# Retention attention with routed experts: another order of the first 20 microseconds (loads, tile moments, first value product, warm-up)

## Chip, cores and metric

One core of one Trainium2 chip. The time is device microseconds of one launch, median of three runs. The matrix work is in float32; the warm-up and the routing one-hots are bfloat16.

## What is computed

Two sequences of 512 tokens with 256 features pass through one layer. Both branches read the normalised input, and both results are added to it:

```
x  = L0_attn_x                       # (2, 512, 256)
xn = _layernorm(x)
# attention: 16 heads of 16, no softmax, a decay per head
q, k, v = heads(xn @ wq.T), heads(xn @ wk.T), heads(xn @ wv.T)
scores = (q @ k.T) * SCALE * gamma_h ** (i - j) * (i >= j)
y = _layernorm(scores @ v, ln_w, ln_b)
attn = (y * silu(xn @ wg.T)) @ wo.T
# experts: 32, four per token, weights 1.8 * softmax(top 4 of the router's logits)
routed = sum_k rw_k * (silu(xn @ gate_e.T) * (xn @ up_e.T)) @ down_e.T
shared = (silu(xn @ sg.T) * (xn @ su.T)) @ sd.T
out = x + attn + routed + shared
```

## The kernel before

The 1024 tokens are 8 tiles of 128, four to a sequence (CPB). The program is written by hand for each engine: every engine runs its own list in order, and semaphores tie the lists together. An instruction that waits holds everything behind it in its own list.

The start. SyncE issues the loads of x in five pieces (HEAD: tile 0, tile 1, then pairs 2-3, 4-5, 6-7; L461), the q/k weights and the v/gate weights (L465, L466), the decay table of 1 MB (`dec`, L469) and the constants (L470). TensorE runs warm-up matmuls on ones (L1353), which produce nothing that is used. VectorE takes each tile's moments (`moments` L924, `aggregate` L927, `scale_moments` L936 and L937), GpSimd raises the variance to the power -1/2 (`token_scale`, L845), VectorE refines the root (L916 to L918) and normalises the tile (L930). Tiles 0 and 1 go one at a time; tiles 2 to 7 have one aggregate, one power and one refinement together. TensorE transposes the normalised tiles (`transpose_tokens`, L1368) and ScalarE copies them to `xnT` (`take_features`, L559).

Each tile t then passes through: `project_qk` (L1430) and `project_vg` (L1440); `scores` (L1455), four PSUM banks r = 0 to 3 with two heads' groups each; `decay_scores` on VectorE (L1095), one product with the decay table for each r; `weigh_values` (L1505), the value product, which reads the decayed scores `st` and the spread values `vz`; `transpose_keys` (L1468) and `decay_keys` (L1102); `chunk_products` (L1481) and `update_state` (L1111) for the state carried to the next tile; `transpose_outputs` (L1514). TensorE interleaves tile t's value product with tile t+1's projections.

GpSimd's list at the start is: two one-tile powers, two memsets, the power for tiles 2 to 7, two casts of constants (L853, L854, after the constants have landed), then `spread_values(0)` (L834), which makes `vz` for tile 0:

```
            token_scale(2, slice(2, NT))
            pool.wait_ge(c2_in, 16)
            nc.gpsimd.tensor_copy(iota_bf[:, :], cst[:, C_IO:C_IO + P])
            nc.gpsimd.tensor_copy(lt_bf[:, :], cst[:, C_LT:C_LT + P]).then_inc(pool_cst, 1)
            spread_values(0)
```

`weigh_values(t)` waits for both of its inputs:

```
                pe.wait_ge(sc_sb, 4 * t + 4)
                pe.wait_ge(vz_sb, 2 * (t + 1))
```

After tile 1's scores come the router's logits over all 1024 tokens (`router_logits`, L1378, which needs all of `xnT`), a ScalarE copy (L573), and two transposes back (`transpose_logits`, L1386). VectorE then picks the experts, and tokens are sorted into blocks beside the attention tiles until about 84 us. The expert pairs run from there to about 178 us, and the weighted sum of the routed rows ends the program.

## Time and profile before

| what | value |
|---|---|
| median of 3 runs | 205.25 us (204.96 to 206.94) |
| profiled execution | 205.5 us |
| its span in the trace | 203.7 us |
| granted TensorE clock | 1.0 of full speed on average |

The trace's time starts with the span. The 1.8 us between the span and the profiled execution's time lie around the program. In rows of the timeline a number after x counts instructions merged into one row, and the bracket gives the engine's idle time before it and what ended it; PE is TensorE's matmuls, PEld its weight loads, DVE VectorE, ACT ScalarE, POOL GpSimd, SPq SyncE's queue. Float32 matmuls appear as several passes, so a row's count can be twice or four times the program's.

### The profile page before, as it was taken

To read this page: it belongs to the slowest core of one execution; us is meant where nothing else is said; L and a number is where in the kernel's file an instruction comes from. 1 tells how busy PE (TensorE), PEld (TensorE's weight loads), DVE (VectorE), ACT (ScalarE), POOL (GpSimd) and SP (SyncE) were. 2 spreads that over 40 slices of the span, in tenths; PEclk is the share of its full clock that TensorE was granted. 3 is DMA by queue.
4 is the path that set the end of the run, shared out by engine and by line. 5 is a ranking of instruction groups with operands and counts; after the bars stand their busy time and mean duration, and the time that the engine had idled before them with its cause. 6 is when DMAs were issued, how large, how long until landed. Compare 5 with 4: busy or idle time off the path is not lost.

```text
span 203.7 us, 4593 instructions
## 1 busy us (share of the span) xinstructions
PE 193.9 (95%) x1594; PEld 143.2 (70%) x1594; DVE 118.6 (58%) x362; ACT 95.1 (47%) x241; POOL 112.1 (55%) x156
## 2 busy tenths in 40 slices
PE   8999998999879999989999999999999999999984
PEld 2666766778466858788888668777866786587653
DVE  2577789798979876764333422433342333415895
ACT  2046247645759242653238547634925931125300
POOL 1234047524984768677777777777777533630000
PEclk9999999999999999999999999999999999999999
DMA  4993999997000029999957334324333333217993
GB/s 124 335 359 130 330 425 427 429 427 344 5 0 0 5 63 393 385 354 396 373 194 266 104 101 146 91 87 146 106 102 105 117 124 142 100 54 237 352 312 131
DMA packets 18551, 42.36 MB, mean 208 GB/s; under 512 B 2517, under 2 KB 11098, under 8 KB 17760
## 3 DMA queue, kind: packets, MB, share of 16 engines
q1 hardware_dynamic: 14640, 33.03, 44.6%
q0 software_dynamic: 3456, 8.92, 13.2%
q8 instruction: 13, 0.21, 0.4%
q10 hardware_dynamic: 432, 0.12, 0.3%
q14 instruction: 10, 0.08, 0.1%
HBM read 34.71 MB, written 7.86 MB: 209 GB/s over the span
## 4 chain that ended last, share of the span: by engine, by line
PE 65%; DVE 10%; POOL 7%; DMA 7%; ACT 4%; issue 4%; SPq 2%; POOLq 0%; DVEq 0%
PE bank L1565 19%; PE bank L1578 6%; DMA w_mem<-y_rows 5%; PE bank L1582 4%; PE bank L1543 4%; PE bank L1353 4%; DVE w_mem L1095 4%; PE bank L1430 4%; PE bank L1440 3%; PE bank L1505 3%; PE bank L1602 3%; PE bank L1455 3%; PE bank L1531 3%; POOL y_rows L823 2%; POOL xg_mem L801 2%
## 5 line engine op out<-in xcount | busy, mean ns | idle before, releaser
L1565 PE MATMUL bank<-xb_mem,w_mem 128*128 128x128 f32 x384 | 47.8, 276 | 0.1
L823 POOL DMA_INDIRECT y_rows<-y_mem,codes x36 | 36.2, 1007 | 18.5 <-DVE y_mem L1158 9.7
L1565 PEld LDWEIGHTS bank<-xb_mem,w_mem 128*128 128x128 f32 x384 | 45.2, 192 | 1.2 <-issue 0.9
L815 POOL DMA_INDIRECT xg_mem<-xn_rows,codes x36 | 35.4, 984 | 12.9 <-issue 9.4
L1150 DVE TENSOR_TENSOR h_mem<-h_mem,bank 128x128 f32<-128x128 f32 x32 | 9.2, 287 | 42.2 <-ACT h_mem L629 41.9
L1095 DVE TENSOR_TENSOR w_mem<-bank,w_mem 128x512 f32<-128x512 f32 x32 | 20.1, 684 | 4.5 <-PE bank L1455 4.4
L1158 DVE COPY y_mem<-bank 128x256 f32<-128x256 f32 x36 | 13.9, 420 | 10.8 <-PE bank L1582 9.5
L628 ACT ACTIVATE h_mem<-bank 128x128 f32<-128x128 f32 x32 | 8.9, 277 | 23.7 <-PE bank L1565 23.4
L641 ACT COPY w_mem<-w_mem 128x1024 f32 x16 | 16.0, 1041 | 3.5 <-PE bank L1620 2.4
L1578 PE MATMUL bank<-w_mem,h_mem 128*128 128x256 f32 x60 | 16.1, 391 | 0.0
L1430 PE MATMUL bank<-w_mem 128*128 128x128 f32 x128 | 15.7, 276 | 0.0
L618 ACT COPY xb_mem<-bank 128x512 f32<-128x512 f32 x16 | 9.3, 584 | 13.6 <-PE bank L1543 12.9
L1430 PEld LDWEIGHTS bank<-w_mem 128*128 128x128 f32 x128 | 15.0, 192 | 0.5 <-issue 0.3
L1440 PE MATMUL bank<-w_mem 128*128 128x512 f32 x32 | 15.1, 593 | 0.0
L1578 PEld LDWEIGHTS bank<-w_mem,h_mem 128*128 128x128 f32 x60 | 10.3, 190 | 4.6 <-DVE h_mem L1152 2.5
L1769 PE MATMUL bank<-xg_mem,ws_mem 128*128 128x256 f32 x48 | 11.1, 385 | 0.0
L567 ACT ACTIVATE w_mem<-bank,cst 128x256 f32<-128x256 f32 x16 | 6.7, 470 | 9.5 <-PE bank L1430 9.4
L772 POOL TENSOR_TENSOR w_mem<-w_mem,cst 128x256 f32<-128x256 f32 x6 | 4.7, 790 | 11.4 <-ACT w_mem L569 11.3
L1582 PE MATMUL bank<-w_mem,h_mem 64*128 64x256 f32 x60 | 10.5, 428 | 0.0
L1543 PE MATMUL bank<-cst,xg_mem 128*128 128x128 f32 x64 | 10.4, 285 | 0.0
L1769 PEld LDWEIGHTS bank<-xg_mem,ws_mem 128*128 128x128 f32 x48 | 8.9, 190 | 2.2 <-issue 0.7
L1304 DVE SCALAR_TENSOR_TENSOR x_sb<-w_mem,rw,x_sb 128x256 f32<-128x256 f32 x22 | 9.4, 480 | 1.5 <-DMA w_mem<-y_rows 1.4
(171 smaller groups left out, 326.0 us busy)
## 6 DMA issues: line engine op xcount, KB each, us to landing
w_mem<-w_exp_dram SPq DMA_DIRECT2D x3, 3456.0 KB, 21.6
w_mem<-w_late_dram SPq DMA_DIRECT2D x7, 1152.0 KB, 7.2
w_mem<-y_rows SPq DMA_DIRECT2D x8, 512.0 KB, 8.0
w_mem<-w_qkvg_dram SPq DMA_DIRECT2D x2, 512.0 KB, 6.2
w_mem<-decay_dram SPq DMA_DIRECT2D x1, 1024.0 KB, 8.2
xn_rows<-w_mem SPq DMA_DIRECT2D x2, 512.0 KB, 3.5
xnt_rows<-w_mem SPq DMA_DIRECT2D x1, 1024.0 KB, 4.9
w_mem<-w_ovf_dram SPq DMA_DIRECT2D x16, 64.0 KB
```

Source lines behind the costliest of these rows:

```text
L641: return nc.scalar.copy(o_mem[:, j * OW:j * OW + XW], w_mem[:, bass.ds(e * EW, XW)])
L815: nc.gpsimd.indirect_dma_start(xg[:, k % RING, :], None, xn_rows, bass.IndirectOffsetOnAxis(ap=codes[:, c, 0:1], axis=0),).then_inc(tok_in ...
L823: nc.gpsimd.indirect_dma_start(y_rows, bass.IndirectOffsetOnAxis(ap=codes[:, c, 1:2], axis=0), ysb[:, k % YRING, :], None, bounds_check=RO ...
L1095: nc.vector.tensor_tensor(st[:, 4 * r * P:4 * (r + 1) * P], ps_s[r][:, :], dec[:, 4 * r * P:4 * (r + 1) * P], ALU.mult).then_inc(sc_sb, 1)
L1158: nc.vector.tensor_copy(ysb[:, w, :], ps[:, 0:D]).then_inc(ys_sb, 1)
L1430: last = nc.tensor.matmul(ps_qk[:, m * P:(m + 1) * P], wqkvg[:, g, m * P:(m + 1) * P], tokens(g, t), start=(g == 0), stop=(g == KT - 1))
L1440: last = nc.tensor.matmul(ps_vg[:, :], tokens(g, t), wqkvg[:, g, 2 * D:4 * D], start=(g == 0), stop=(g == KT - 1))
L1543: last = nc.tensor.transpose(ps_xt[p % 2][:, (2 * g + j) * P:(2 * g + j + 1) * P], xg[:, k % RING, g * P:(g + 1) * P], ident)
L1565: last = nc.tensor.matmul(ps_gu[j][:, m * P:(m + 1) * P], w[:, o:o + P], xbT[:, p % 2, (2 * g + j) * P:(2 * g + j + 1) * P], start=(g == 0 ...
L1578: nc.tensor.matmul(ps_dn[j][:, 0:D], hA[:, 2 * (p % 2) + j, :], w[:, j * EW + KT * MB:j * EW + XW], start=True, stop=False)
L1582: nc.tensor.matmul(ps_dn[j][:, 0:D], hC[rows, p % 2, :], w2[rows], start=False, stop=True).then_inc(dn_ps, 1)
L1769: last = nc.tensor.matmul(to, ws_mem[:, o:o + P], xnT_back[:, g, n], start=(g == 0), stop=(g == KT - 1))
```

## The change

- Warm-up: 17 matmuls become 15 ahead of the first transposes, and behind them 5 (17 // 3) become 2 (15 // 7).
- SyncE issues the decay table after tiles 2-3 of x, ahead of tiles 4 to 7.
- VectorE takes the moments of tiles 2 and 3, then decays the score banks 0 and 1 of tile 0, then does the moments of tiles 4 to 7 with the aggregates and scales of tiles 2 to 7, then banks 2 and 3, then the refinement and all six normalisations.
- TensorE does the first value product and tile 0's key transposes ahead of the transposes of tiles 2 to 5; tiles 6-7 are transposed behind tile 1's scores; the router's logits go behind the chunk products.
- The transposes of tiles 2 to 7 write other PSUM banks, with waits to match. Two waits for feature copies ahead of the value product and the key transposes go.
- ScalarE's list follows: its three feature copies stand together behind `take_outputs(0)`.

GpSimd's list is not touched.

```diff
--- before.py
+++ after.py
@@ -58,7 +58,7 @@
 DVE_ROWS = {n: (0, 1, 2, 3) for n in range(5)} | {5: (2, 3)}
 PE_ROWS = ((5, 0), (5, 1), (6, 0), (6, 1), (6, 2), (6, 3), (7, 0), (7, 1), (7, 2), (7, 3))
 PE_TILES = (5, 6, 7)
-WARM_UP = 17
+WARM_UP = 15
 CT = 32
 
 
@@ -297,7 +297,7 @@
         bank = [ctx.enter_context(nc.psum_tensor(f"bank{i}", [P, 512], F32)) for i in range(8)]
         ps_tr, ps_qk, ps_vg, ps_sg, ps_s0, ps_s1, ps_y, ps_po = bank
         ps_s = [ps_s0, ps_s1, ps_sg, ps_tr]
-        ps_f = [ps_s0, ps_s1, ps_y, ps_po, ps_qk]
+        ps_f = [ps_s0, ps_s1, ps_qk, ps_vg, ps_qk]
 
         ps_xt, ps_gu, ps_dn, ps_og, ps_ot = [ps_qk, ps_vg], [ps_s0, ps_s1], [ps_sg, ps_tr], ps_y, ps_po
         ps_sa, ps_sc, ps_sd = ps_xt, ps_gu, [ps_dn, [ps_og, ps_ot]]
@@ -464,9 +464,10 @@
             tokens_in(1)
             sp.dma_start(wqkvg[:, :, 0:2 * D], w_qkvg[:, :, 0:2 * D]).then_inc(wqk_in, 16)
             sp.dma_start(wqkvg[:, :, 2 * D:4 * D], w_qkvg[:, :, 2 * D:4 * D]).then_inc(wvg_in, 16)
-            for u in range(2, len(HEAD)):
-                tokens_in(u)
+            tokens_in(2)
             sp.dma_start(dec[:, :], decay).then_inc(d_in, 16)
+            tokens_in(3)
+            tokens_in(4)
             sp.dma_start(cst[:, C_BM:C_END], consts[:, C_BM:C_END]).then_inc(c2_in, 16)
             sp.dma_start(wo[:, :, :], w_out).then_inc(w_in, 16)
             sp.dma_start(lnw[:, :], lnwb[0].partition_broadcast(P)).then_inc(w_in, 16)
@@ -692,16 +693,14 @@
                     take_output_tokens(t - 1)
                 hot_positions(t, "tok")
                 take_queries_keys(t + 1)
-                if t == 0:
-                    take_features(2)
-                    take_features(3)
                 if t >= 2:
                     take_transposed(t - 2)
                 hot_positions(t, "z")
                 take_values_gate(t + 1)
                 take_outputs(t)
                 if t == 0:
-                    take_features(4)
+                    for u in range(2, len(HEAD)):
+                        take_features(u)
                 if t == T_RANK + 1:
                     hot_positions(t, "y")
                 if 1 <= t < T_EXPERT:
@@ -946,13 +945,17 @@
             normalise(0)
             refine(1, slice(1, 2))
             normalise(1)
-            for t in range(2, NT):
-                last = moments(t)
-            step(last)
-            for t in range(2, NT):
-                last = aggregate(t)
-            step(last)
-            scale_moments(slice(2, NT))
+            moments(2)
+            step(moments(3))
+
+            def rest_of_moments():
+                for t in range(4, NT):
+                    last = moments(t)
+                step(last)
+                for t in range(2, NT):
+                    last = aggregate(t)
+                step(last)
+                scale_moments(slice(2, NT))
 
             def take_logits():
                 dve.wait_ge(lg_ps, 1)
@@ -1205,13 +1208,12 @@
                         make_codes()
                         find_block_experts()
                     decay_scores(t, r)
-                    if t == 0 and r == 0:
-                        refine(2, slice(2, NT))
-                        for u in range(2, 6):
-                            normalise(u)
+                    if t == 0 and r == 1:
+                        rest_of_moments()
                 if t == 0:
-                    normalise(6)
-                    normalise(7)
+                    refine(2, slice(2, NT))
+                    for u in range(2, NT):
+                        normalise(u)
                 if t == T_RANK - 1:
                     take_logits()
                 if t % CPB > 0 and t < NT - 1:
@@ -1360,8 +1362,12 @@
             def transpose_tokens(u):
 
                 pe.wait_ge(xn_done, HEAD[u][-1] + 1)
+                if u == 2:
+                    pe.wait_ge(qk_sb, 2)
+                if u == 3:
+                    pe.wait_ge(vg_sb, 4)
                 if u == 4:
-                    pe.wait_ge(qk_sb, 2)
+                    pe.wait_ge(xnT_sb, 3)
                 for g in range(KT):
                     for j, t in enumerate(HEAD[u]):
                         o = (len(HEAD[u]) * g + j) * P
@@ -1459,8 +1465,6 @@
                             last.then_inc(sc_ps, 1)
 
             def transpose_keys(t):
-                if t == 0:
-                    pe.wait_ge(xnT_sb, 4)
                 if t >= 2:
                     pe.wait_ge(res_sb, t - 1)
                 need(pe, st_sb, states_before(t))
@@ -1493,8 +1497,6 @@
                                      qd[:, t % 2, g * P:(g + 1) * P], start=(g == 0), stop=False, skip_group_check=True)
 
             def weigh_values(t):
-                if t == 0:
-                    pe.wait_ge(xnT_sb, 3)
                 pe.wait_ge(sc_sb, 4 * t + 4)
                 pe.wait_ge(vz_sb, 2 * (t + 1))
                 for g in range(KT):
@@ -1683,7 +1685,7 @@
                     transpose_back(NT - 1)
 
             transpose_tokens(0)
-            warm_up(WARM_UP // 3)
+            warm_up(WARM_UP // 7)
             pe.wait_ge(xnT_sb, 1)
             pe.wait_ge(wqk_in, 16)
             project_qk(0)
@@ -1698,7 +1700,7 @@
                 if t >= 1:
                     scores(t)
                 if t == 1:
-                    router_logits()
+                    transpose_tokens(4)
                 if t == T_INVERT:
                     route_inverse()
                 if not more:
@@ -1706,6 +1708,8 @@
                     transpose_pair(0)
                 if t % CPB > 0:
                     chunk_products(t - 1)
+                if t == 1:
+                    router_logits()
                 if t >= 1:
                     transpose_outputs(t - 1)
                 if t == 1:
@@ -1723,16 +1727,14 @@
                 if t >= 2 and more:
                     transpose_back(t - 2)
                 from_state(t)
-                if t == 0:
-                    transpose_tokens(2)
-                    transpose_tokens(3)
                 if t >= 2 and more:
                     project_out(t - 2)
                 weigh_values(t)
                 if t % CPB < CPB - 1:
                     transpose_keys(t)
                 if t == 0:
-                    transpose_tokens(4)
+                    transpose_tokens(2)
+                    transpose_tokens(3)
 
             pe.wait_ge(vg_sb, 2 * NT)
             transpose_pair(1)
```

TensorE, from tile 1's v/gate projection to the logits' transposes, before:

```order
L1440 MATMUL bank<-w_mem 128x512 x2
L1368 MATMUL bank<-cst,w_mem 128x128 x8
L1505 MATMUL bank<-w_mem 32x128 x16
L1468 MATMUL bank<-cst,w_mem 128x128 x2
L1368 MATMUL bank<-cst,w_mem 128x128 x4
L1455 MATMUL bank<-w_mem 128x256 x8
L1378 MATMUL bank<-w_mem 32x256 x8
L1481 MATMUL bank<-w_mem 128x128 x2
L1514 MATMUL bank<-cst,w_mem 128x128 x2
L1386 MATMUL bank<-cst,w_mem 128x128 x2
```

The same stretch of TensorE's list in the changed kernel (L1446 is the v/gate projection, L1507 the value product, L1472 the key transposes, L1374 the transposes of x, L1461 scores, L1485 chunk products, L1384 logits, L1516 outputs, L1392 logits back):

```order
L1446 MATMUL bank<-w_mem 128x512 x2
L1507 MATMUL bank<-w_mem 32x128 x16
L1472 MATMUL bank<-cst,w_mem 128x128 x2
L1374 MATMUL bank<-cst,w_mem 128x128 x8
L1461 MATMUL bank<-w_mem 128x256 x8
L1374 MATMUL bank<-cst,w_mem 128x128 x4
L1485 MATMUL bank<-w_mem 128x128 x2
L1384 MATMUL bank<-w_mem 32x256 x8
L1516 MATMUL bank<-cst,w_mem 128x128 x2
L1392 MATMUL bank<-cst,w_mem 128x128 x2
```

The eight transposes of tiles 2 to 5 moved from ahead of the value product to behind it, the four of tiles 6-7 to behind the scores, and the logits to behind the chunk products.

VectorE, from the moments of tile 2 to tile 0's decayed keys, before:

```order
L924 BN_STATS w_mem<-x_sb 128x6 x6
L927 BN_AGGR w_mem<-w_mem 128x2 x6
L936 TENSOR_SCALAR w_mem<-w_mem 128x6
L937 TENSOR_SCALAR w_mem<-w_mem 128x6
L1095 TENSOR_TENSOR w_mem<-bank,w_mem 128x512
L916 TENSOR_TENSOR w_mem<-w_mem 128x6
L917 TENSOR_TENSOR w_mem<-w_mem 128x6
L918 SCALAR_TENSOR_TENSOR w_mem<-w_mem 128x6
L930 TENSOR_SCALAR w_mem<-x_sb,w_mem 128x256 x4
L1095 TENSOR_TENSOR w_mem<-bank,w_mem 128x512 x3
L930 TENSOR_SCALAR w_mem<-x_sb,w_mem 128x256 x2
L1102 TENSOR_TENSOR w_mem<-bank,cst 128x256
```

The same stretch in the changed kernel (L923 moments, L1098 decays, L926 aggregates, L935 and L936 scales, L915 to L917 the refinement, L929 the normalisations):

```order
L923 BN_STATS w_mem<-x_sb 128x6 x2
L1098 TENSOR_TENSOR w_mem<-bank,w_mem 128x512 x2
L923 BN_STATS w_mem<-x_sb 128x6 x4
L926 BN_AGGR w_mem<-w_mem 128x2 x6
L935 TENSOR_SCALAR w_mem<-w_mem 128x6
L936 TENSOR_SCALAR w_mem<-w_mem 128x6
L1098 TENSOR_TENSOR w_mem<-bank,w_mem 128x512 x2
L915 TENSOR_TENSOR w_mem<-w_mem 128x6
L916 TENSOR_TENSOR w_mem<-w_mem 128x6
L917 SCALAR_TENSOR_TENSOR w_mem<-w_mem 128x6
L929 TENSOR_SCALAR w_mem<-x_sb,w_mem 128x256 x6
L1105 TENSOR_TENSOR w_mem<-bank,cst 128x256
```

Two decays now stand ahead of the aggregates and scales, and no normalisation stands between the decays.

## Rows read from the trace of the kernel before

**Rows 1.** The page, part 4: engines on the chain that ended last.

```profile
PE 65%; DVE 10%; POOL 7%; DMA 7%; ACT 4%; issue 4%; SPq 2%; POOLq 0%; DVEq 0%
```

**Rows 2.** Timeline, TensorE, start to first projection: start us, us, engine, line, op.

```profile
0.96 6.78 PE L1353 MATMUL bank<-w_mem 128*128 128x512 bf16 x17 [0.96 <-POOL w_mem L839]
...
6.91 0.34 PEld L1353 LDWEIGHTS bank<-w_mem 128*128 128x128 bf16 x2 [0.28 <-issue]
...
7.58 0.38 PE L1368 MATMUL bank<-cst,w_mem 128*128 128x128 f32 x2
...
7.80 1.24 PE L1353 MATMUL bank<-w_mem 128*128 128x512 bf16 x5
...
8.88 1.95 PE L1430 MATMUL bank<-w_mem 128*128 128x128 f32 x16
```

**Rows 3.** Timeline, TensorE, from the first scores to tile 2's projection.

```profile
12.69 1.15 PE L1455 MATMUL bank<-w_mem 32*128 32x256 f32 x16
...
17.37 1.04 PE L1368 MATMUL bank<-cst,w_mem 128*128 128x128 f32 x8
...
18.65 1.09 PE L1505 MATMUL bank<-w_mem 128*32 128x128 f32 x32 [0.24 <-ACT w_mem L559]
...
19.94 0.60 PE L1368 MATMUL bank<-cst,w_mem 128*128 128x128 f32 x4
...
20.47 1.15 PE L1455 MATMUL bank<-w_mem 32*128 32x256 f32 x16
...
21.55 1.07 PE L1378 MATMUL bank<-w_mem 128*32 128x256 f32 x16
...
23.10 0.38 PE L1514 MATMUL bank<-cst,w_mem 128*128 128x128 f32 x2
...
23.53 1.95 PE L1430 MATMUL bank<-w_mem 128*128 128x128 f32 x16
```

**Rows 4.** Timeline, VectorE.

```profile
9.65 2.29 DVE L924 BATCH_NORM_STATS2 w_mem<-x_sb 128x6 f32<-128x256 f32 x6 [1.86 <-DMA x_sb<-x_dram]
...
13.96 0.69 DVE L1095 TENSOR_TENSOR w_mem<-bank,w_mem 128x512 f32<-128x512 f32 x1 [1.20 <-PE bank L1455]
...
15.24 1.38 DVE L930 TENSOR_SCALAR w_mem<-x_sb,w_mem 128x256 f32<-128x256 f32 x4
...
21.64 2.48 DVE L1095 TENSOR_TENSOR w_mem<-bank,w_mem 128x512 f32<-128x512 f32 x4 [1.07 <-PE bank L1455]
...
29.14 0.42 DVE L1102 TENSOR_TENSOR w_mem<-bank,cst 128x256 f32<-128x256 f32 x1 [0.56 <-PE bank L1468]
```

**Rows 5.** Timeline, GpSimd, from the third power to the first value spread.

```profile
12.91 1.33 POOL L845 TENSOR_TENSOR w_mem<-w_mem 128x6 f32<-128x6 f32 x1 [6.17 <-DVE w_mem L937]
...
14.89 0.29 POOL L853 CAST w_mem<-cst 128x128 bf16<-128x128 f32 x1 [0.65 <-DMA cst<-consts_dram]
...
15.37 0.76 POOL L834 COPY w_mem<-w_mem 128x128 f32<-128x128 f32 x2
```

**Rows 6.** Timeline, ScalarE, three copies out of PSUM.

```profile
8.00 0.37 ACT L559 COPY w_mem<-bank 128x256 f32<-128x256 f32 x1 [5.37 <-PE bank L1368]
...
20.58 0.58 ACT L559 COPY w_mem<-bank 128x512 f32<-128x512 f32 x1 [0.40 <-PE bank L1368]
...
22.68 0.37 ACT L573 COPY w_mem<-bank 128x256 f32<-128x256 f32 x1 [1.52 <-PE bank L1378]
```

**Rows 7.** Timeline, SyncE's queue: two of the loads issued at the start.

```profile
1.63 0.68 SPq L465 DMA_DIRECT2D w_mem<-w_qkvg_dram  x1
...
5.68 0.66 SPq L469 DMA_DIRECT2D w_mem<-decay_dram  x1
```

**Rows 8.** The page, part 6: DMA issues, KB each, median us to landing.

```profile
w_mem<-w_qkvg_dram SPq DMA_DIRECT2D x2, 512.0 KB, 6.2
...
w_mem<-decay_dram SPq DMA_DIRECT2D x1, 1024.0 KB, 8.2
```

**Rows 9.** Timeline, TensorE: its longest idle stretch before 66 us.

```profile
57.41 0.44 PE L1468 MATMUL bank<-cst,w_mem 128*128 128x128 f32 x2 [1.60 <-DVE x_sb L1126]
```

## The prediction

> **What bounds the kernel now.** I read the chain that ended last first: 65% of it is TensorE [rows 1]. Then I read the timeline of the first 30 us engine by engine, since the whole change lies there. TensorE's rows run nearly end to end: warm-ups and projections [rows 2], then scores at 12.69, transposes at 17.37, the first value product at 18.65, and so on to tile 2's projection at 23.53 [rows 3]. The reader should see that almost no row of TensorE has an idle time in its bracket; the one with 0.24 us is the first value product, held by a ScalarE copy. Last, VectorE sits idle for 0.56 us at 29.14 until TensorE's key transposes of tile 1 arrive [rows 4], and the routing work hangs on VectorE from there. So what TensorE loses or gains before 29 us goes into the end. I measure each case by when tile 2's projection starts, 23.53 before.
>
> **The start, 0.73 us earlier.** From 0.96 to 7.58 TensorE issues 17 matmuls of 512 columns [rows 2]. At 1.2 GHz one takes 0.427 us, at 2.4 GHz 0.213 us; 6.62 us are 14 at the lower clock and 3 at the upper. So the two that go would have run at the upper clock: 0.43 us, and the transposes start at 7.15. Tile 0 is normalised by then, since its copy would otherwise not have followed the transposes so closely: it starts 0.42 us after them and takes 0.37 [rows 6]. Now 7.15 + 0.42 + 0.37 = 7.94, and with some 0.2 for the signal and the weight load the first projection starts at 8.15. Before it started at 8.88, right behind the five warm-ups of 7.80 [rows 2]; two of them now end at 7.8 and don't hold it. Its weights were issued at 1.63 [rows 7] and land 6.2 us later [rows 8], at 7.8: just in time. Gain 8.88 - 8.15 = 0.73. Scores of tile 0 move from 12.69 to 11.96.
>
> **The decay load.** Issued at 5.68 [rows 7], it lands after 8.2 us [rows 8], at 13.88, and the first decay starts at 13.96 [rows 4]. Tile 1's decays start 1.17 us after its scores (20.47 to 21.64, [rows 3, 4]), so tile 0's could have started at 13.86. The load cost only 0.1 before, but with scores 0.73 earlier it would eat the gain. Ahead of 512 KB of x it lands sooner: the last tiles of x had landed when their moments were taken, about 11.2 (9.65 + 4 x 0.38), so the table behind them took 2.7 us to 13.88; counted from 9.65, when tiles 2-3 are in [rows 4], it is there by about 12.4. I take it as no longer late. Tiles 4 to 7 then land by 13.9 at the latest, the end of the same bytes before, and are wanted at 14.4.
>
> **The new wait.** The value product needs the spread values. The spread stands on GpSimd behind the power for tiles 2 to 7, and that power needs the moments of all of them [rows 5]. Before, this was done at 15.37 + 0.76 = 16.13, well ahead of TensorE. Now the moments of tiles 4 to 7 come behind two decays. Step by step:
> - first decay at 11.96 + 1.17 = 13.13; two decays at 2.48/4 = 0.62 each [rows 4]: 14.37
> - four moments at 2.29/6 = 0.38 [rows 4]: 15.90
> - aggregates, scales and the signal: from the moments' end before, 9.65 + 2.29 = 11.94, to the power at 12.91 [rows 4, 5], 0.97: 16.87
> - the power, 1.33: 18.20. The two casts, 15.37 - 14.89 = 0.48, with the constants long landed, plus 0.05: 18.73
> - the spread, 0.76 [rows 5]: 19.49, and 0.1 for the signal: the value product starts at 19.6, against 18.65.
>
> TensorE is through tile 1's projections at 17.37 - 0.73 = 16.64, so it stands still for nearly 3 us with the transposes, the scores and all else queued behind it. VectorE's banks 2 and 3, done at 16.9 + 1.25 = 18.1, are not the last wait. That is +0.95.
>
> **From the value product to tile 2's projection.** Before this took 23.53 - 18.65 = 4.88 [rows 3]. Now the transposes of tiles 2 to 5 are in it: eight transposes at 0.11 us, since the four of 19.94 are done some 0.44 later, ahead of the scores at 20.47 [rows 3]: +0.88. Are their inputs ready at about 20.8? The refinement starts with the power's end, 18.3, and takes under 0.7; normalisations go at 1.38/4 = 0.35 each [rows 4]: tile 3 at 19.7, tile 5 at 20.4, tile 7 at 21.1. Yes, by a few tenths; this costs nothing.
>
> Tiles 6-7 are transposed behind tile 1's scores. Before, transposes at 19.94 led to a copy at 20.58 of 0.58 [rows 3, 6], hidden under the scores. Now the logits come only the chunk products later: the copy's end is 0.64 + 0.58 + 0.05 = 1.27 after the transposes' start, and transposes and chunk products fill 0.44 + 0.5 (from 21.55 to 23.10 are logits and chunk products, 1.55, less 1.05). Wait +0.33. The logits' own copy ends 22.68 + 0.37 - 21.55 = 1.50 after the logits start, with the signal 1.65; before, chunk products and output transposes covered it, now logits and output transposes fill 1.05 + 0.22. Wait +0.38. Bounds of the two together: 0 if they stay hidden, 1.0 if ScalarE is late with them; I take 0.71, which the rows give.
>
> **Sum.** 0.95 + 0.88 + 0.33 + 0.38 = +2.54 at tile 2's projection; the gain of 0.73 and the lost 0.24 stall are already in the 0.95. VectorE's path to 29 us is late too, but less: the logits reach it at about 26.3 instead of 24.04, +2.3. So TensorE's +2.54 holds at 29.14 and is carried on. The profiled execution, 205.5, becomes 208.0; it lies 0.25 over the median, so the median becomes 207.8. Bounds of the new wait: GpSimd's spans are called rough by the page. If they are much too long, VectorE's fourth decay at 18.1 is the last wait, the value product starts at 18.2 and the sum is 1.1. If normalisations or spread slow each other, another 0.5 comes on top.
>
> **Rivals.**
> (a) The wait is small: GpSimd's chain is really a microsecond or more shorter, or the two copies stay hidden. For it: the power of six columns was never on the chain, so its true end is bounded only by VectorE's use of it. Against it: a decrease of more than 1.4 us is not to be had. Result +1.1 to +1.9, 206.4 to 207.1: within 1%. It decides if the spread ends before 19.0.
> (b) TensorE's clock falls in the gap. The longest idle stretch before 66 us is 1.60 us [rows 9], and what follows it runs at the upper of the two levels; the new gap is nearly 3 us, which no row here covers. If the clock fell and stayed down as long as at the start (0.96 to about 6.9, 5.9 us), the work in that time would run at half speed: at most +3.0, together 210.8. The Trainium skill (TensorE: Matmul & The Clock Gate, "Why this matters for your kernels") warns that idle gaps between bursts of matmuls bring the clock back to its half rate. By that rule the sum would be 210.8; the trace agrees only in that shorter gaps do no harm.
> (c) Not slower: the delay is taken up behind 29 us and the earlier start stays. For that VectorE or TensorE would have to have some 2.5 us of slack in the routing stage. TensorE has idle time there, 1.60 us at 57.41 [rows 9], and if the same work could slide into it, and the last waits there were not for this stage's start, the kernel would come out at 205.25 - 0.73 = 204.5. It decides from the point at which VectorE stops being fed late. Against it: the chain runs through VectorE's idle 0.56 us at 29.14 straight to TensorE, and later idle times are waits for VectorE's own chain, which shifts with it.
> (d) The change doesn't do what it says: the value product is first on TensorE's list, but isn't first in time since it still waits for the moments. That is what I forecast. If instead its inputs were there when TensorE comes, at 16.7, tile 2's projection would start at 16.7 + 4.88 + 0.88 + 0.71 = 23.17, 0.4 early: 204.9. The fourth decay at 18.1 alone excludes that.
>
> **How the numbers follow.** The forecast (+2.0 to +3.3) gets 0.65, (a) 0.2, (b) 0.1, (c) and (d) together 0.05. Both of these end within 1% too; a gain of over 1% has no mechanism here, and 0.02 is left for it. A measurement of this kernel tells about 1%, 2.05 us, from no change: the line is 207.3. Within the forecast some 0.05 lies under the line, the rest above; with (b) slower is 0.70, within 1% is 0.28, faster 0.02. The range goes from 206.4, the low end of (a), to 210.2, over half of (b).
>
> **What would show it.** In the changed trace: first projection near 8.2; first decay near 13.1; the power on GpSimd near 16.9, the spread's end near 19.5; the value product at 19.6 with an idle bracket of nearly 3 us that names GpSimd; logits with 0.3 us of idle and the logits' transposes with 0.4; tile 2's projection near 26.1; VectorE's decayed keys of tile 1 near 31.7; everything behind by 2.5. I am wrong if the value product starts before 18.7, if matmuls behind the gap take twice their time, or if the later stages don't shift with the first.

## The result, and the profile after

| | before | changed |
|---|---|---|
| median | 205.4 us (6 runs, 204.96 to 206.94) | 209.24 us (6 runs, 207.43 to 209.46) |
| ratio | | 1.0172, interval 1.0138 to 1.0206 |
| profiled execution, its span | 205.5, 203.7 | 209.17, 207.3 |

The changed kernel is slower by 1.7%. Ratios, here and below, leave out executions more than 1.5% above the fastest of their kernel; medians and ranges keep them. The timeline of the changed kernel on TensorE, with the columns of [rows 2] and [rows 3]:

```profile
0.96 5.53 PE L1355 MATMUL bank<-w_mem 128*128 128x512 bf16 x15 [0.96 <-POOL w_mem L838]
...
6.80 0.41 PE L1374 MATMUL bank<-cst,w_mem 128*128 128x128 f32 x2 [0.31 <-DVE w_mem L929]
...
7.67 2.05 PE L1436 MATMUL bank<-w_mem 128*128 128x128 f32 x16
...
11.58 1.15 PE L1461 MATMUL bank<-w_mem 32*128 32x256 f32 x16
...
18.82 1.87 PE L1507 MATMUL bank<-w_mem 128*32 128x128 f32 x32 [2.39 <-POOL w_mem L833]
...
21.10 1.65 PE L1374 MATMUL bank<-cst,w_mem 128*128 128x128 f32 x8
...
22.69 1.15 PE L1461 MATMUL bank<-w_mem 32*128 32x256 f32 x16
...
25.14 1.07 PE L1384 MATMUL bank<-w_mem 128*32 128x256 f32 x16 [0.28 <-issue]
...
26.69 0.44 PE L1392 MATMUL bank<-cst,w_mem 128*128 128x128 f32 x2
...
26.97 1.95 PE L1436 MATMUL bank<-w_mem 128*128 128x128 f32 x16
```

The first projection starts at 7.67 (8.88 before, [rows 2]), the first scores at 11.58 (12.69, [rows 3]): the start did get faster, by 1.21 and 1.11 us. Then the value product stands behind 2.39 us of idle time that the row puts down to GpSimd's L833, the value spread. The value product starts at 18.82, hardly later than the 18.65 of before. But tile 2's projection starts at 26.97 against 23.53. And one row is odd: the same 32 passes of the value product take 1.87 us, where before they took 1.09 [rows 3].

VectorE, which answers to [rows 4]:

```profile
12.81 1.29 DVE L1098 TENSOR_TENSOR w_mem<-bank,w_mem 128x512 f32<-128x512 f32 x2 [2.86 <-PE bank L1461]
...
14.02 1.39 DVE L923 BATCH_NORM_STATS2 w_mem<-x_sb 128x6 f32<-128x256 f32 x4
...
18.49 2.44 DVE L929 TENSOR_SCALAR w_mem<-x_sb,w_mem 128x256 f32<-128x256 f32 x6
...
32.57 0.42 DVE L1105 TENSOR_TENSOR w_mem<-bank,cst 128x256 f32<-128x256 f32 x1 [1.29 <-PE bank L1472]
```

The first two decays, then the four moments without a wait, so both the table and tiles 4 to 7 had landed. The normalisations end only at 20.9. VectorE's key decay of tile 1 stood at 29.14 before and stands at 32.57 now, with 1.29 us of idle time in place of 0.56. I call this row "the keys" and use it as the measure of the first stage below: +3.43.

GpSimd, which answers to [rows 5]:

```profile
16.38 1.33 POOL L844 TENSOR_TENSOR w_mem<-w_mem 128x6 f32<-128x6 f32 x1 [9.87 <-DVE w_mem L936]
...
17.67 0.28 POOL L852 CAST w_mem<-cst 128x128 bf16<-128x128 f32 x1
...
18.15 0.52 POOL L833 COPY w_mem<-w_mem 128x128 f32<-128x128 f32 x2
```

The power runs at 16.38 (12.91 before), and the spread behind it at 18.15 (15.37 before). Last, busy time in four stretches, the start and three around the gap: us, each engine's busy time, TensorE's granted clock (PEclk), DMA.

```profile
core 0: us, PE busy (x) PEld busy (x) DVE busy (x) ACT busy (x) POOL busy (x), PEclk, DMA share, GB/s
0.00:5.40 5.40, 4.44 (x11) 1.64 (x12) 1.97 (x11) 1.50 (x3) 1.41 (x8) 1.00 0.53 139
...
16.30:18.80 2.50, 0.13 (x1) 0.01 (x1) 2.07 (x6) 0.66 (x2) 2.42 (x6) 1.00 0.00 0
...
18.80:22.60 3.80, 3.78 (x42) 3.33 (x42) 2.56 (x7) 0.77 (x2) 1.32 (x3) 0.55 0.55 181
...
22.60:26.90 4.30, 3.91 (x46) 2.54 (x45) 2.48 (x4) 1.99 (x5) 0.00 (x0) 1.00 0.52 198
```

In the 2.5 us ahead of the value product TensorE was all but idle. In the 3.8 us behind it, the granted clock was 0.55 of full speed, which is the lower of the two levels, 1.2 GHz, for nearly all of that stretch, and then 1.00 again. In the kernel before no stretch up to 28.7 us shows less than 1.00. The column is to be read beside durations: it says 1.00 for the first 5.4 us too, where 11 warm-ups took 4.44 us, 0.40 each, nearly the prediction's 0.427 for the lower level. Behind the gap column and durations agree (1.87 against 1.09). The six executions of the changed kernel show this too: five have a mean clock of 0.99 (0.990 to 0.992) and take 209.17 to 209.46 us; the sixth has 0.999 and takes 207.43.

So there are two parts: work that starts late, and a clock that is down behind the gap.

### The profile page after: what moved, and what is told of

The parts are those of the page before. It is cut to its first block, busy times and chain, and to the rows that moved or that the text cites. A ratio compares the mean times of both kernels' runs of the same rounds, so it can differ in the third digit from the quotient of the medians.

```text
span 207.3 us, 4585 instructions
## 1 busy us (share of the span) xinstructions
PE 194.3 (94%) x1589; PEld 143.8 (69%) x1589; DVE 118.8 (57%) x362; ACT 95.4 (46%) x241; POOL 112.3 (54%) x156
## 4 chain that ended last, share of the span: by engine, by line
PE 69%; DVE 16%; POOL 6%; ACT 4%; issue 2%; DMA 1%; ACTq 0%; DVEq 0%; POOLq 0%
PE bank L1567 20%; PE bank L1580 7%; PE bank L1771 5%; PE bank L1584 5%; DVE w_mem L1098 4%; PE bank L1545 4%; PE bank L1507 3%; PE bank L1604 3%; PE bank L1436 3%; PE bank L1461 3%; DVE x_sb L1306 3%; PE bank L1446 2%; PE bank L1533 2%; POOL xg_mem L800 2%; ACT xg_mem L585 2%
## 5 line engine op out<-in xcount | busy, mean ns | idle before, releaser
L1098 DVE TENSOR_TENSOR w_mem<-bank,w_mem 128x512 f32<-128x512 f32 x32 | 20.1, 683 | 7.2 <-PE bank L1461 7.1
L1580 PE MATMUL bank<-w_mem,h_mem 128*128 128x256 f32 x60 | 16.1, 392 | 0.0
L1446 PE MATMUL bank<-w_mem 128*128 128x512 f32 x32 | 15.1, 593 | 0.0
L1580 PEld LDWEIGHTS bank<-w_mem,h_mem 128*128 128x128 f32 x60 | 10.3, 190 | 4.6 <-DVE h_mem L1155 2.5
L1507 PE MATMUL bank<-w_mem 128*32 128x128 f32 x256 | 9.5, 292 | 2.7 <-POOL w_mem L833 2.4
L1507 PEld LDWEIGHTS bank<-w_mem 128*32 128x32 f32 x256 | 7.2, 115 | 5.4 <-issue 4.8
```

The source lines that it names most:

```text
L1098: nc.vector.tensor_tensor(st[:, 4 * r * P:4 * (r + 1) * P], ps_s[r][:, :], dec[:, 4 * r * P:4 * (r + 1) * P], ALU.mult).then_inc(sc_sb, 1)
L1446: last = nc.tensor.matmul(ps_vg[:, :], tokens(g, t), wqkvg[:, g, 2 * D:4 * D], start=(g == 0), stop=(g == KT - 1))
L1507: last = nc.tensor.matmul(ps_y[CT * r:CT * (r + 1), g * P:(g + 1) * P], vz[:, t % 2, h * CT:(h + 1) * CT], st[:, s * P:(s + 1) * P], start ...
L1580: nc.tensor.matmul(ps_dn[j][:, 0:D], hA[:, 2 * (p % 2) + j, :], w[:, j * EW + KT * MB:j * EW + XW], start=True, stop=False)
```

## The experiments

Each changes one thing in the changed kernel (names that begin with a) or in the kernel before (b); x are mixtures. "Value product", "projection" (tile 2's) and "keys" (VectorE's key decay of tile 1) are start times in the profiled execution.

| kernel | value product | projection | keys | median us | ratio to before |
|---|---|---|---|---|---|
| before | 18.65 | 23.53 | 29.14 | 205.2 | |
| changed | 18.82 | 26.97 | 32.57 | 209.2 | 1.0172 |
| a_spread_first | 17.61 | 26.88 | 32.49 | 207.66 | 1.0130 (1.0091 to 1.0169) |
| a_fill_gap | 18.84 | 25.39 | 30.99 | 208.47 | 1.0161 (1.0118 to 1.0203) |
| a_moments_early | 17.69 | 24.84 | 30.45 | 207.14 | 1.0094 (1.0068 to 1.0120) |
| a_old_loads | 19.39 | 27.56 | 33.16 | 209.82 | 1.0211 (1.0156 to 1.0265) |
| b_warm_loads | 21.56 | 26.44 | 32.05 | 209.30 | 1.0179 (1.0135 to 1.0223) |
| b_warm | 18.23 | 23.12 | 28.73 | 205.11 | 1.0001 (0.9963 to 1.0040) |
| b_loads | 21.11 | 27.54 | 33.15 | 210.50 | 1.0222 (1.0154 to 1.0289) |
| x_order | 16.24 | 22.81 | 28.42 | 205.77 | 1.0017 (0.9996 to 1.0038) |
| a_spread_fill2 | 17.65 | 25.52 | 31.12 | 208.50 | 1.0164 (1.0094 to 1.0234) |

### The spread ahead of the power (a_spread_first)

```diff
+            spread_values(0)
             token_scale(2, slice(2, NT))
             pool.wait_ge(c2_in, 16)
...
-            spread_values(0)
```

> The changed kernel with one edit: GpSimd spreads tile 0's values ahead of the power for tiles 2 to 7. Theory (the value product is held by GpSimd's list, and TensorE's clock falls in the gap): the spread is done by about 13, the value product now waits only for the fourth decay and starts at 17.4 to 17.6 instead of 18.8, the idle stretch ahead of it shrinks from 2.4 us to about 1.2, the granted clock stays at 1.0, and the transposes of tiles 2 and 3 wait some tenths for their normalisation. Time 206.3 to 207.0, some 1.5 us over the kernel before. Rival (the loss comes from the transposes and logits standing later on TensorE's list, and the gap is only where it shows): 208.5 to 209.2.

Measured 207.66, and on TensorE, in a view that ends at 21 us (so five of the eight transposes' passes):

```profile
17.61 1.09 PE L1507 MATMUL bank<-w_mem 128*32 128x128 f32 x32 [1.05 <-DVE w_mem L1098]
...
18.63 0.44 PE L1472 MATMUL bank<-cst,w_mem 128*128 128x128 f32 x2
...
19.95 1.31 PE L1374 MATMUL bank<-cst,w_mem 128*128 128x128 f32 x5 [0.89 <-DVE w_mem L929]
```

The value product is released by VectorE's decay at 17.61, as expected, and runs at full speed. But the transposes of tiles 2 and 3 now wait 0.89 us for a normalisation, and in the profiled execution the clock fell there, at 20.0 (1.83 us for tile 1's scores, 1.08 before): the profiled execution took 209.19, with a mean clock of 0.992, the other three 207.56 to 207.66 with 1.0. The median lies between the two forecasts, 0.7 above the theory's 206.3 to 207.0 and 0.8 below the rival's 208.5. The three executions with the clock held compare with the 207.43 of the changed kernel's one such execution: no gain. And with the clock held by fill, the keys come at 30.99 without this edit and at 31.12 with it (a_fill_gap and a_spread_fill2, below): the spread's place on GpSimd by itself is worth nothing. The late power holds the normalisations just as it held the spread, and the wait moves by one step. The gain in the median goes with the clock, which was down in one of four executions here and in five of six in the changed kernel. That is too few to show that two short gaps bring it down less often than one long gap.

### Matmuls in the gap (a_fill_gap)

```diff
+                if t == 0:
+                    warm_up(11)
                 weigh_values(t)
```

> The changed kernel with 11 warm-up matmuls of 512 columns (2.35 us at the upper clock) put ahead of tile 0's value product, where TensorE stood still for 2.4 us. They write a bank that the value product then starts anew. Theory (the gap lets the clock fall): the value product still starts at 18.8, but the granted clock holds 1.0 from there on, the 32 passes of the value product take 1.09 us instead of 1.87, and the time is 207.3 to 207.7, some 1.6 us under the changed kernel. Rival (the passes behind the gap are long for another reason, such as memory traffic of the normalisations beside them): 209.0 to 209.6, with the same long passes.

The chain of work that ended last (start us, us, what), four pieces:

```profile
16.46 2.37 PE bank L1355 x11
...
18.84 1.09 PE bank L1507 x32
...
20.30 0.87 PE bank L1374 x8
...
30.99 0.42 DVE w_mem L1105
```

and the stretch behind the gap, with the columns of the changed kernel's above:

```profile
18.80:22.60 3.80, 3.79 (x63) 3.06 (x63) 2.84 (x8) 1.45 (x3) 1.35 (x3) 1.00 0.54 179
```

The clock is 1.00, the value product takes 1.09, the eight transposes' passes 0.87 (in the changed kernel's chain 1.45), and the keys come at 30.99, 1.58 us earlier than in the changed kernel. Only fill was added, so the idle gap is what the lower clock goes with, and the price is 1.6 us, close to the 1.8 between the two kinds of executions of one kernel (209.2 and 207.4). One of the four executions, 209.86, still has a mean clock of 0.992; no trace shows where it fell.

The time missed its bracket of 207.3 to 207.7: it was 208.47, and the ratio, 1.0161, is not told apart from the changed kernel's 1.0172. In the profiled execution the keys' gain is there, but TensorE then loses 0.8 us of it in the expert stage, in two steps:

```profile
85.85 0.63 PE L1545 MATMUL bank<-cst,xg_mem 128*128 128x128 f32 x4 [0.43 <-issue]
...
174.25 0.42 DVE L1161 COPY y_mem<-bank 128x256 f32<-128x256 f32 x1 [0.67 <-DMA y_rows<-y_mem,codes]
...
174.82 1.10 PE L1580 MATMUL bank<-w_mem,h_mem 128*128 128x256 f32 x4 [0.16 <-DVE y_mem L1161]
```

The same pair of VectorE's copies in the changed kernel, without a wait for a DMA between them:

```profile
174.35 0.76 DVE L1161 COPY y_mem<-bank 128x256 f32<-128x256 f32 x2 [1.16 <-PE bank L1584]
```

Counted from the inversion of the routing (TensorE's L1418, 69.93 here, 71.49 in the changed kernel), TensorE's rows come 0.38 us later than the changed kernel's from 86 us on, and 0.77 later from 174.8 on. The second step is a VectorE copy of an expert result that waits for the write of an earlier result to `y_rows`, and TensorE's L1580 waits for that copy.

### The moments in their old place (a_moments_early)

```diff
-            moments(2)
-            step(moments(3))
-
-            def rest_of_moments():
-                for t in range(4, NT):
+            for t in range(2, NT):
...
-                    if t == 0 and r == 1:
-                        rest_of_moments()
```

> The changed kernel with VectorE's moments, aggregates and scales of tiles 2 to 7 all ahead of the first decay again, as before the change; TensorE's new order, loads and warm-up stay. Theory (the moved moments are what holds the value product): the spread is done at about 16, the value product starts at 16.3 to 16.5 with no idle time, tile 2's projection at about 22.8 against 23.5 before; time 204.3 to 205.0. Rival (TensorE's new order costs by itself, through the extra work ahead of tile 2's projection and the two exposed copies): 206 to 207.

Measured 207.14, 2.1 us over the top of the theory's bracket, with the clock held in all four executions (0.998 or 1.0). VectorE and TensorE (a view that ends at 20 us):

```profile
12.79 1.48 DVE L923 BATCH_NORM_STATS2 w_mem<-x_sb 128x6 f32<-128x256 f32 x4 [2.48 <-DMA x_sb<-x_dram]
...
17.69 1.09 PE L1501 MATMUL bank<-w_mem 128*32 128x128 f32 x32 [1.17 <-POOL w_mem L833]
...
19.33 0.97 PE L1368 MATMUL bank<-cst,w_mem 128*128 128x128 f32 x5 [0.18 <-DVE w_mem L929]
```

VectorE waits 2.48 us for tiles 4 and 5 of x, until 12.79. Before the change the six moments ran from 9.65 without a wait [rows 4]. The loads, not the moments' place, make it late: the decay table now goes ahead of these tiles. With the clock held on both sides this edit gains little: 207.14 against 207.43, and 30.45 against 30.99 at the keys.

### Warm-up and loads in the kernel before (b_warm_loads), and each alone (b_warm, b_loads)

```diff
-WARM_UP = 17
+WARM_UP = 15
...
-            for u in range(2, len(HEAD)):
-                tokens_in(u)
+            tokens_in(2)
             sp.dma_start(dec[:, :], decay).then_inc(d_in, 16)
+            tokens_in(3)
+            tokens_in(4)
...
-            warm_up(WARM_UP // 3)
+            warm_up(WARM_UP // 7)
```

> The kernel before with only the shorter warm-up and the decay table loaded ahead of tiles 4 to 7. Theory (the start is worth what TensorE's list shows, 0.7 to 1.2 us, and is carried to the end): 204.2 to 204.7. Rival (a wait that comes back takes the gain, such as a load or the decays): 205.2 to 205.5.

It took 209.3, which neither side expected: two edits that I had taken for gains, and as slow as the whole change. Its four executions go from 208.44, with a mean clock of 0.999, to 211.88 with 0.976. The profiled one is that with the clock held, although TensorE stood idle for 2.24 and 1.18 us in it, with 1.3 us of transposes between: the late tiles, without the clock, make it 3.2 us slower. The two were then run apart, with the hunk of the loads alone and that of the warm-up alone.

> The kernel before with the shorter warm-up alone. Theory (the load order is what cost 3 us when warm-up and loads were changed together): no harm; the first projection starts 0.7 to 1.2 us earlier, but the decay table still lands at 13.9, the first decay stays there and the value product starts at 18.3 to 18.6, so the time is 204.8 to 205.3. Rival (the shorter warm-up is what cost, since the matrix engine starts its work too soon or at a lower clock): 207 to 209.

> The kernel before with the decay table loaded ahead of tiles 4 to 7 alone. Theory: tiles 4-5 land at 12.8 to 13.3 instead of before 10.5, VectorE, which takes their moments ahead of everything, stands still for some 2.5 us, the six normalisations and the transposes behind them come late, tile 2's projection starts at 26 to 26.5; time 207.8 to 208.6. Rival (warm-up to blame): 205.1 to 205.6.

b_loads, at 210.5:

```profile
12.86 1.49 DVE L925 BATCH_NORM_STATS2 w_mem<-x_sb 128x6 f32<-128x256 f32 x4 [2.51 <-DMA x_sb<-x_dram]
...
18.63 1.30 PE L1369 MATMUL bank<-cst,w_mem 128*128 128x128 f32 x8 [1.77 <-DVE w_mem L931]
...
21.11 1.94 PE L1506 MATMUL bank<-w_mem 128*32 128x128 f32 x32 [1.18 <-ACT w_mem L560]
```

Moments 2.51 us late for want of x, transposes late by 1.77 us of idle time, and behind them the value product again at the lower clock (1.94 us). It is 1.9 us over the bracket of 207.8 to 208.6; I had not counted the clock, which accounts for most of it by the price found above. In the profiled execution (211.02, a mean clock of 0.983) the clock was down a second time, behind a gap of the same length as the one of [rows 9]:

```profile
61.46 0.44 PE L1469 MATMUL bank<-cst,w_mem 128*128 128x128 f32 x2 [1.60 <-DVE x_sb L1127]
...
61.83 1.87 PE L1456 MATMUL bank<-w_mem 32*128 32x256 f32 x16
```

The scores take 1.87 us here and 1.15 in the kernel before, and the granted clock is 0.54 from 61.8 to 65.5 us. b_warm, at 205.11:

```profile
7.82 2.05 PE L1430 MATMUL bank<-w_mem 128*128 128x128 f32 x16
...
13.67 0.69 DVE L1095 TENSOR_TENSOR w_mem<-bank,w_mem 128x512 f32<-128x512 f32 x1 [1.01 <-DMA w_mem<-decay_dram]
...
18.23 1.09 PE L1505 MATMUL bank<-w_mem 128*32 128x128 f32 x32 [0.78 <-ACT w_mem L559]
```

The first projection is 1.06 us earlier, but the first decay waits for the table (DMA), and the value product for ScalarE; 0.42 us is left at the value product, 0.41 at the keys, and nothing that can be measured at the end. So the warm-up is harmless and worth nothing that the medians show, and the load order alone costs as much as the whole change where VectorE wants tiles 4 to 7 first (1.0222 against 1.0172, with intervals that overlap).

### The changed kernel with the old loads (a_old_loads)

The hunk of the loads taken back.

> The changed kernel with the decay table loaded behind tiles 4 to 7, as before. Theory: the first decay starts at 13.9 instead of 12.8, and since the moments, the power and the spread follow it, the value product starts at 19.9 behind a gap of 3.6 us, with the clock fallen; time 210.0 to 210.6. Rival (the load order is hidden either way): 209.0 to 209.5.

```profile
13.38 1.29 DVE L1097 TENSOR_TENSOR w_mem<-bank,w_mem 128x512 f32<-128x512 f32 x2 [3.22 <-DMA w_mem<-decay_dram]
...
19.39 1.09 PE L1506 MATMUL bank<-w_mem 128*32 128x128 f32 x32 [3.10 <-POOL w_mem L832]
...
22.46 1.96 PE L1460 MATMUL bank<-w_mem 32*128 32x256 f32 x16
```

Measured 209.82, 0.2 below the bracket. The first decay does wait for the table, 13.38 instead of 12.81, and the gap is 3.10 us. The clock fell again, though not at once: the value product has its 1.09 us, tile 1's scores take 1.96. So with the moments late, the early table is worth 0.6 us at the keys (32.57 against 33.16, both with the clock down; in the times, 209.2 and 209.8, the intervals overlap); with the moments early it costs, as a_moments_early and b_loads show. The load order and the moments' place have to be chosen together.

### TensorE's order with the old loads and moments (x_order, x_hidden)

x_order is the changed kernel with the loads and the moments back in their old places, and the spread ahead of the power; TensorE's order and the short warm-up stay.

> The changed kernel's warm-up and TensorE order, with the loads and VectorE's moments in their old places and the value spread ahead of the power on GpSimd. Theory (each wait of the changed kernel comes from the loads, the moved moments and GpSimd's queue; TensorE's order itself costs the two exposed copies of 0.7 us): the moments are through at 12.5, the value product waits for the fourth decay and starts at 16.5, the granted clock stays at 1.0, tile 2's projection at about 23.1; time 204.5 to 205.2. Rival (TensorE's order costs 1.5 us by itself): 206 to 206.8.

The chain, three pieces:

```profile
14.59 1.72 PE bank L1439 x4
...
16.31 1.02 PE bank L1500 x32
...
28.42 0.42 DVE w_mem L1100
```

No gap at all: TensorE goes from tile 1's projections straight into the value product at 16.3, and the keys are at 28.42, 0.72 us ahead of the kernel before. The first stage went as the theory had it (the projection 0.3 early). The time did not: 205.77, not told apart from the kernel before, and 0.6 over the top of the bracket. From the keys on, this kernel takes some 0.2 us longer to the inversion of the routing (38.97 us against 38.72). The rest isn't lost in the profiled execution, which at 205.10 is the fastest of the ten: the shared experts' first matmul comes at 177.46 against 177.91, and the span is 203.2 against 203.7. What makes the other nine slower (205.42 to 205.99, clocks of 0.998 to 1.0) no trace shows.

This run takes out the late moments, the loads and the spread's place together, so it shows that they hold nearly the whole loss, and not the share of each. For TensorE's new order it leaves at most some tenths (1.0017, interval 0.9996 to 1.0038).

x_hidden also put the transposes of tiles 6-7 and the logits back where they were.

> The kernel of the run x_order with the transposes of tiles 6-7 ahead of tile 1's scores and the logits ahead of the chunk products, as before the change, so that ScalarE's two copies are covered again. Theory (the changed TensorE order costs 0.7 us in exposed copies): tile 2's projection starts at 22.1 to 22.3 instead of 22.8, VectorE's key decay of tile 1 at 27.8 to 28.0 against 29.1 in the kernel before; time 204.2 to 204.9, 0.3 to 0.8 us under the kernel before. Rival (gains of the first 30 us don't reach the end): 205.0 to 205.7.

The keys came at 28.39, no earlier than in x_order: the copies are covered again, but the transposes wait for the normalisations instead, and the gain is gone. Its time (231.17) says nothing, since the chip of this batch ran every kernel some 26 us longer, with stops behind 78 us, the kernel before included (231.9); the first 31 us of the profiles of this batch agree with those of other chips.

### Fill again (a_fill_8, a_spread_fill, a_spread_fill2)

a_fill_8 has 8 matmuls where a_fill_gap has 11; a_spread_fill is a_spread_first with 5 ahead of the value product and 4, to another PSUM bank, ahead of the transposes.

> The changed kernel with 8 warm-up matmuls (1.7 us) ahead of the value product, where 11 stood before: TensorE stands still for about 0.7 us of the 2.4. Clock theory: that is enough, the granted clock stays at 1.0 behind the gap, the value product's 32 passes take 1.09 us, VectorE's key decay of tile 1 starts at 31.0 to 31.1 instead of 32.6, and the time is 207.4 to 207.9. If the 11 matmuls cost something by themselves in the first run of this kind (208.5 where 207.5 was expected), 8 cost less of it. Rival (only an unbroken stretch keeps the clock): 208.8 to 209.3.

> The changed kernel with the values spread ahead of the power on GpSimd, and TensorE's two idle stretches that this left (1.05 us ahead of the value product, 0.89 us ahead of the transposes of tiles 2 and 3) filled with 5 and 4 warm-up matmuls. Clock theory: with the spread alone the clock still fell at 20.0, so filled stretches give back some 1.6 us there; tile 2's projection starts at 25.3 to 25.5 instead of 26.9, time 206.0 to 206.7. Rival (the late normalisations set the pace, not the clock): 207.4 to 207.8.

Both ran in the batch just named (234.97 and 233.63 us). Up to the keys both did what the clock theory said: with 0.67 us idle left in the gap the granted clock stayed at 1.00 and the keys came at 31.02; with the two gaps of a_spread_first filled they came at 30.92 instead of 32.49. The second was run again on another chip.

> The kernel of a_spread_fill once more, since the chip of that batch ran every kernel, the one before too, some 26 us longer by stops behind 78 us. The first 31 us of that run agreed with the clock theory: key decay of tile 1 at 30.92, 1.57 us ahead of the same kernel without the fills. On a chip that runs the kernel before in 205.2: 206.6 to 207.1, and no execution with the clock fallen. Rival (the 1.57 us don't reach the end): 207.5 or more.

Keys at 31.12, value product at 17.65. The time is 208.5, a miss: the rival's side. One of its four executions, 209.58, has a mean clock of 0.992; the other three, with the clock held, took 207.89 to 208.65. The 1.4 us at the keys don't reach the end. The shared experts' first matmul comes 110.7 us after the inversion of the routing, as in a_fill_gap (110.8), and 110.05 both in the kernel before and in the changed one. So both profiled executions with fill lose 0.7 to 0.8 us in the expert stage. In this one it goes in a single step, the one at 174.8 found in a_fill_gap: VectorE's copy at 174.26 waits 0.91 us for the write to `y_rows`, and TensorE's L1578 behind it 0.40 us. No profiled execution without fill on a chip that ran the kernel before in 205 us has this wait. What delays that write, and whether the fill does, stays open.

## Why the prediction was right, and where it was off

The forecast was 207.8, slower, by one wait: the value product held through GpSimd's list by moments taken late. The row of the value product names that releaser. The direction and the late power behind it are right: the power starts 3.5 us later than before, and with the moments and loads put back and the spread moved ahead of it the loss is gone (x_order). But the spread is only one of two things that hang on that power. Moved ahead of it, it gained nothing at the held clock, since the normalisations wait for the same power (a_spread_first).

That the time lay in the range is partly luck. The forecast's own band, +2.0 to +3.3, holds neither the delay without the clock, +1.85 at the keys, nor the whole, +3.8 in the medians. The first was below it and the clock's 1.6 us carried the sum past it; the range held 209.24 only because it reached over half of rival (b). And one of the prediction's three signs of being wrong came true: matmuls behind the gap took nearly twice their time. Point by point:

- **The start.** Forecast 0.73 us earlier at the first projection, measured 1.21. The first tile landed 0.24 us sooner, though nothing ahead of its load was changed, and 15 warm-ups took 5.53 us, so they were out of the way. How long they take differs by execution, with the moment at which the clock rises: 4.80 in a_fill_gap and 6.06 in a_spread_first, with the first transposes at 6.82 and 6.92. That alone doesn't reach the end (b_warm).
- **The load.** "No longer late", and tiles 4 to 7 wanted after they land: right for this order of VectorE (12.81 and no wait at 14.02). I did not see how much hung on it: with the moments ahead of the decays it costs 2.5 us of waiting.
- **The new wait.** Forecast 19.6, measured 18.82: +0.17 instead of +0.95 at the value product. Of the 0.78 between them 0.38 is the earlier start of the scores, and 0.24 the spread, which took 0.52 instead of 0.76; the rest is in VectorE's steps. The power took the 1.33 us read from the row before.
- **From the value product on.** Forecast +0.88, +0.33, +0.38. At the held clock (a_fill_gap) from 18.84 to 25.39 it is 6.55, against 4.88 before: +1.67, forecast +1.59. Right. The two waits are 0.28 (the bracket at 25.14) and 0.35 (the weight load at 26.69, which names ScalarE). The first names no releaser, but ScalarE's copy of tiles 6-7 ends at 25.03, just ahead of it.
- **Sum.** Without the clock, +1.85 at the keys (30.99 against 29.14), forecast +2.54; the difference is the 0.78 at the value product, less 0.08 behind it.
- **Rival (b), the clock.** This is the step that failed: it was left out of the sum, and got a chance of 0.1 and a price of up to 3.0. It came in five of six executions, at a gap of 2.39 us, for 1.6 us. I had argued from the longest gap before, 1.60 us [rows 9], after which nothing fell in that execution. One execution was too little to carry a chance of 0.1: in b_loads the clock did fall behind a gap of 1.60 us at the same place. 1.85 and 1.58 make the 3.43 at the keys; with the 0.2 us from there to the inversion (38.92 against 38.72) that is the 3.6 in the spans. The page of the Trainium skill that I named, "TensorE: Matmul & The Clock Gate", section "Why this matters for your kernels", warns that an idle gap between bursts of matmuls brings the clock back to its half rate. The trace agrees in kind: 0.55 granted behind the gap. The gap here is shorter than the ones that the page warns of, and the measurement decides.
- **Rival (a), a small wait,** has the number without the clock: +1.85 lies in its +1.1 to +1.9, and by its own sign it decides, since the spread ended at 18.67, before 19.0. Its mechanism was not there: from the power's start to the spread's end GpSimd took 2.29 us, forecast 2.62, not a microsecond less, and the copies were exposed. **Rival (c), slack behind 29 us,** is out for delays: +3.43 at the keys is +3.6 at the end. For gains it is open: 0.41 and 0.72 us earlier at the keys (b_warm, x_order) show no gain in the medians, but in the profiled executions the spans are 203.3 and 203.2 against 203.7.

No kernel run here beats the one before.

## What to carry to other kernels

When an instruction moves back on one engine, follow what it feeds through the lists of the other engines: here six tiles' moments fed a power, and behind that power, on GpSimd's list, stood an unrelated copy that the matrix engine needed. Then look for everything else that hangs on the late instruction before moving the copy: here the next wait took its place. A load moved forward displaces others, and whether it gains depends on which engine wants those first: the same edit was worth 0.6 us in one order and cost a wait of 2.5 us in another. And price a new gap on TensorE twice, once for its length and once for the clock behind it.

## What I had not expected of the hardware

- The length of a gap did not decide. Gaps of 1.05 and 0.89 us, 1.5 us of work apart, also brought the clock down, but in one of four executions (a_spread_first); one of 2.39 us did in five of six; with 0.67 us left of it (a_fill_8) the granted clock was 1.00 up to the keys in the profiled execution. Behind 1.60 us it stayed up in the profiled execution of the kernel before and fell in that of b_loads; behind 2.24 and 1.18 us it stayed up in that of b_warm_loads, and behind 1.77 and 1.18 us at the same two places it fell in that of b_loads.
- The kernel before is not free of it: of 19 executions beside b_warm and x_order, two had a mean clock of 0.991 or 0.992 and took 206.97 and 206.8 us, where the median was 205.17. The same 1.7 us. Where it fell in them no trace shows.
- The lower clock didn't begin at the gap's end in every kernel: in a_old_loads the value product ran at full speed behind 3.10 us of idle time, and the transposes and scores after it ran at half.
